# A first pass with constant mask rows and own scores apart, with four smaller edits, in a transformer block on one core

## The reference, in short

```
h = layernorm(x)*(1+ca) + sa
q, k, v = h @ w_qkv.T + b            # 16 heads of 8 dims
lines   = normalised exterior products of 4-dim projections (write: h[t-1], h[t]; read: h[t], h[t])
logits  = q.k/sqrt(8) + <read_line_q, J write_line_k> * decay_h**(q-k) * bias_scale_h   (second term for q > k)
x = x + ga * (softmax_causal(logits) @ v @ w_out.T + b_out)
h = layernorm(x)*(1+cb) + sb
x = x + gb * (top-2 of 8 experts, each 128 -> 256 (SwiGLU) -> 128, weighted by a softmax over the two)
```

## Time and profile before

| | us |
|---|---|
| three runs | 1112.86, 1106.92, 1110.35 |
| median | 1110.35 |
| profiled execution | 1111.9 |
| its span | 1110.2 |
| mean granted clock of TensorE | 0.955 |

### The profile page before, as it was taken

How to read it: one execution, slowest core, us unless ns; L and a number is a source line. 1 busy time by engine, 2 the same in 40 slices (tenths; PEclk the granted TensorE clock), 3 DMA queues, 4 the chain that set the end, 5 groups by cost and what they waited for, 6 DMA issues and landing times. The chain is left out here.

```text
span 1110.2 us, 30824 instructions
## 1 busy us (share of the span) xinstructions
PE 935.1 (84%) x9473; PEld 742.2 (67%) x9473; DVE 775.5 (70%) x2067; ACT 721.6 (65%) x1612; POOL 811.7 (73%) x1352
## 2 busy tenths in 40 slices
PE   2346899889999899998999989998872799999967
PEld 2335677767777777777777777776652688888852
DVE  8576668777777777777777777777746466555536
ACT  2435678887778877888787887876562455555520
POOL 8366668888888888888888888887435366666644
PEclk9997999999999999999999999998985899999989
DMA  7336556565666656666566665655411353333339
GB/s 189 114 110 161 150 139 172 152 178 137 168 159 158 172 147 160 161 158 173 143 163 159 153 178 146 163 156 157 118 44 49 79 168 93 91 91 91 83 138 357
DMA packets 233854, 160.39 MB, mean 144 GB/s; under 512 B 57376, under 2 KB 220512, under 8 KB 233568
## 3 DMA queue, kind: packets, MB, share of 16 engines
q1 hardware_dynamic: 222416, 133.77, 46.0%
q0 software_dynamic: 8448, 17.45, 5.1%
q10 hardware_dynamic: 2832, 7.20, 1.7%
HBM read 81.38 MB, written 76.19 MB: 142 GB/s over the span
## 5 line engine op out<-in xcount | busy, mean ns | idle before, releaser
L919 DVE TENSOR_REDUCE peak<-pre 128x6 f32<-128x768 f32 x256 | 244.5, 955 | 116.4 <-PE pre L759 113.5
L1151 ACT ACTIVATE PT<-sc 128x768 f32<-128x768 f32 x256 | 204.6, 799 | 35.3 <-PE sc L746 32.9
L950 DVE TENSOR_TENSOR sc<-sc,decay 128x512 f32<-128x512 f32 x256 | 177.5, 693 | 30.4 <-PE sc L730 25.3
L1637 POOL DMA_INDIRECT yab<-y_out,xt x136 | 131.4, 966 | 82.8 <-issue 63.4
L1359 POOL DMA_INDIRECT xg<-stage,slot_i x128 | 130.9, 1022 | 62.9 <-issue 26.8
L759 PE MATMUL pre<-causal,identb 128*128 128x256 bf16 x512 | 144.7, 283 | 0.0
L758 PE MATMUL pre<-KT,queries 84*128 84x256 bf16 x512 | 143.5, 280 | 0.0
L757 PE MATMUL pre<-KT,queries 84*128 84x128 bf16 x512 | 116.5, 228 | 20.4 <-DMA queries<-line_rows 12.6
L1591 DVE TENSOR_TENSOR hid<-silu,up 128x256 f32<-128x256 f32 x136 | 57.3, 421 | 82.0 <-ACT silu L1545 82.0
L743 PE MATMUL sc<-queries,KT 99*128 99x128 bf16 x512 | 101.6, 223 | 13.2 <-issue 6.8
L1545 ACT ACTIVATE silu<-up 128x256 f32<-128x256 f32 x136 | 52.2, 384 | 88.4 <-PE up L1481 88.4
(11 more groups left out here) (279 smaller groups left out, 2731.9 us busy)
## 6 DMA issues: line engine op xcount, KB each, us to landing
line_rows<-line_part SPq DMA_DIRECT2D x64, 216.0 KB
dim_rows<-dim_part SPq DMA_DIRECT2D x64, 192.0 KB, 2.1
KT<-dim_rows SPq DMA_DIRECT2D x64, 192.0 KB
queries<-dim_rows SPq DMA_DIRECT2D x64, 192.0 KB
line_rows<-line_part SPq DMA_DIRECT2D x64, 144.0 KB
KI<-line_rows SPq DMA_DIRECT2D x64, 144.0 KB
QI<-line_rows SPq DMA_DIRECT2D x64, 144.0 KB
xt<-xg SPq DMA_DIRECT2D x136, 65.0 KB, 1.9
```

The costliest lines, as they stand in the source:

```text
L919: nc.vector.reduce_max(peak[half][:, i:i + 2, 0:3], pre[:, :, 0:3 * P].rearrange("p n (g k) -> p n g k", g=3), AX.X)\
L950: nc.vector.tensor_tensor(seeded(p), seeded(p), decay[:, 2 * p:2 * p + 2, :].unsqueeze(2).broadcast_to([P, 2, NT, P]), ALU.mult).then_inc( ...
L1151: nc.scalar.activation(PT[p % 4][:], sc[:, window], ACT.Exp).then_inc(exped.sem, 1)
L1637: nc.gpsimd.indirect_dma_start(yab, bass.IndirectOffsetOnAxis(xt[r][:, D:D + 1].bitcast(i32), 0), y_out[r % 8][:], None).then_inc(y_sent[r ...
```

## The change

1. **First pass.** A new pair of tiles KB and QB (`first_rows`, not doubled by batch parity) holds 64 constant mask rows, set in the setup, and 48 rows of dims, loaded per half. The two diagonal blocks are products of QB and KB over these 112 rows; the block of later queries against earlier keys stays a product of QF and KT over rows 0:84. A head takes 3 x 128 columns; the matmul with the mask is gone. The score of a token with itself, which the mask rows leave out, is computed apart: DVE multiplies q and k (`own_part`, in attnT's tile, slot 4), a new job "self" (slot 6) sums the dims of a head by two small products with `head_of`, and DVE copies them beside the maxima (slot 7). `peak` has three tiles, and the last maximum (`peak_top`) runs over three values for both halves of the queries.
2. **Loads.** load_rows has two more DMAs of 192 KB, ahead of the four, and holds until the whole half's first pass is done. The peaks' rows are 84:87 of QF instead of 96:99.
3. **Residual.** Job res is two transposes; DVE adds the PSUM to x_all; ACT's copy is gone.
4. **Squares** run behind all evacuations of ACT's slot 4.
5. **Setup.** Six fills by DVE become two of half the length; POOL's fills of KT are fewer or half as long, its causal mask is gone; DVE has a second cast (KB beside KI), both early; ACT copies QB's mask rows.
6. **Pads.** The tile lies in first_rows and is filled by POOL behind the loop; the DMAs wait for it.

```diff
-    (6, 0, "back", -2, 1), (6, 1, "max0", 1, 0),
+    (6, 0, "back", -2, 1), (6, 1, "max0", 1, 0), (6, 2, "self", 3, 1),
...
                 for m in range(2):
-                    nc.vector.memset(v["KT"][m][32:64].rearrange("p h t -> p (h t)").bitcast(u32), 0)
-                    nc.vector.memset(v["QF"][m][32:64].rearrange("p h t -> p (h t)").bitcast(u32), 0)
-                    nc.vector.memset(v["QF"][m][64:96].rearrange("p h t -> p (h t)").bitcast(u32), 0)
+                    nc.vector.memset(pairs(v["QF"][m])[0:PEAK0, :, 0:P // 2], 0)
...
+                dve.wait_ge(key_mask_ok, 1)
+                for tile in ("KI", "KB"):
+                    nc.vector.tensor_copy(v[tile][0:MR].rearrange("p h (t k) -> p (h t) k", t=NT),
+                                          key_mask[1][:].unsqueeze(1).broadcast_to([MR, H * NT, P]))
...
-                    hold(pre_ready, jb - 1, 4 * half + 1)
+                    hold(pre_ready, jb - 1, 4 * half + 4)
                     heads, done = slice(8 * half, 8 * half + 8), rows_loaded[half].sem
+                    for kq, tile in ((0, KB), (1, QB)):
+                        sp.dma_start(tile[MR:PRE, heads, :], dim_rows[jb % 3][kq, :, heads, :]).then_inc(done, 16)
...
                 iterations(sp, body)
+                sp.wait_ge(pads_made, 2)
                 sp.dma_start(xg[E * CAP:XROWS, :].rearrange("(n p) d -> p n d", p=P), pads[:, 8:16, :]).then_inc(padded, 16)
...
-                        nc.tensor.matmul(pre[:, n, 0:P], QF[par][0:DIMS + LINES, h, 0:P], KT[par][0:DIMS + LINES, h, 0:P], start=True, stop=False)
-                        nc.tensor.matmul(pre[:, n, P:3 * P], QF[par][0:DIMS + LINES, h, P:T], KT[par][0:DIMS + LINES, h, :], start=False, stop=False)
-                        last = nc.tensor.matmul(diagonal(pre, n), identb[:], causal[:].unsqueeze(1).broadcast_to([P, 2, P]),
-                                                start=False, stop=True)
+                        first, second = slice(0, P), slice(P, T)
+                        nc.tensor.matmul(pre[:, n, 0:P], QB[0:PRE, h, first], KB[0:PRE, h, first], start=True, stop=True)
+                        nc.tensor.matmul(pre[:, n, P:T], QF[par][0:PEAK0, h, second], KT[par][0:PEAK0, h, first], start=True, stop=True)
+                        last = nc.tensor.matmul(pre[:, n, T:3 * P], QB[0:PRE, h, second], KB[0:PRE, h, second], start=True, stop=True)
...
                         wait(pe, used["out"], jb)
-                        settle(pe, pe_settled)
                         for t in range(NT):
                             blk = slice(t * P, (t + 1) * P)
-                            nc.tensor.matmul(B[:, blk], ident[:], x_all[:, span(jb * T + t * P, P)], start=True, stop=False)
-                            last = nc.tensor.matmul(B[:, blk], yT[:, blk], ident[:], start=False, stop=True)
+                            last = nc.tensor.transpose(B[:, blk], yT[:, blk], ident[:])
...
+                    elif name == "self":
+                        wait(pe, own_ready, jb)
+                        for t in range(NT):
+                            last = nc.tensor.matmul(B[:, t * H:(t + 1) * H], own_part[:, t * P:(t + 1) * P], head_of[:],
+                                                    start=True, stop=True)
...
                             if pp % 4 == 3:
                                 wait(dve, maxed, pb, 4 * half + 4)
-                                nc.vector.reduce_max(peak[half][:, :, 3], peak[half][:, :, 1:3], AX.X).then_inc(peaked.sem, 1)
+                                wait(dve, peak_step, pb - 1, 2 * half + 2)
+                                nc.vector.reduce_max(peak_top[half][:], mine[:, 8 * half:8 * half + 8], AX.X).then_inc(peaked.sem, 1)
...
+                    if p == 7 and live(b + 3):
+                        jb = b + 3
+                        wait(dve, ready["self"], jb)
+                        wait(dve, peaked, jb - 3, 2)
+                        own = bank[BANK["self"]][:, 0:NT * H].rearrange("p (t h) -> p h t", h=H)
+                        nc.vector.tensor_copy(peak[jb % 3][:].rearrange("p h t k -> p h (t k)")[:, :, 1:6:4], own)\
+                          .then_inc(used["self"].sem, 1)
...
                         jb = b + 3
+                        wait(dve, used["kq"], jb)
+                        wait(dve, ready["self"], jb - 1)
+                        wait(dve, ready["out"], jb - 4)
+                        nc.vector.tensor_tensor(own_part[:], dim_val[:, 0, :], dim_val[:, 1, :], ALU.mult).then_inc(own_ready.sem, 1)
                         wait(dve, squares, jb)
...
+                        wait(dve, ready["res"], jb)
+                        rows = x_all[:, span(jb * T, T)]
+                        nc.vector.tensor_tensor(rows, rows, bank[BANK["res"]][:, 0:T], ALU.add).then_inc(used["res"].sem, 1)
...
-                        if p == 4 and live(b + 3):
-                            squared(b + 3)
                         if p == 0 and live(b - 1):
...
                         if p == 4 and live(b - 2):
                             evacuate("norm2", b - 2, par)
+                        if p == 4 and live(b + 3):
+                            squared(b + 3)
...
                 iterations(pool, body)
+                wait(pool, pre_ready, NB - 1)
+                nc.gpsimd.memset(pads[:], 0.0).then_inc(pads_made, 1)
+                pool.wait_ge(pads_made, 1)
+                nc.gpsimd.iota(pads[:, :, D:D + 1].bitcast(i32), pattern=[[P, 16], [0, 1]], base=2 * NB * T,
+                               channel_multiplier=1).then_inc(pads_made, 1)
```

More of the change, by code:

```diff
@@ L33 @@
 INC = MR + LINES
+PRE = MR + DIMS
 LW = T + P
@@ L194, in build @@
         QI = a("QI", [P, H, T], bf16)
+        first_rows = a("first_rows", [P, 2, H, T], bf16)
+        KB, QB = (first_rows[:, n] for n in range(2))
+        pads = first_rows[:].rearrange("p n h t -> p (n h t)").bitcast(fp32)[:, 0:16 * ROW].rearrange("p (n d) -> p n d", d=ROW)
+        head_of = a("head_of", [P, H])
         VP = [a(f"VP{n}", [P, NT, H, 32]) for n in range(2)]
@@ L273, in _ @@
                                         pattern=[[-1, P]], channel_multiplier=1).then_inc(ident_ok, 1)
+                nc.gpsimd.memset(query_mask[0][:], MASK)
+                step(nc.gpsimd.memset(key_mask[0][:], 1.0))
+                nc.gpsimd.affine_select(out=key_mask[1][:], in_=key_mask[0][:], compare_op=ALU.is_ge, fill=0.0, base=-1,
+                                        pattern=[[1, P]], channel_multiplier=-2).then_inc(key_mask_ok, 1)
                 step(nc.gpsimd.iota(dist_i[:], pattern=[[1, P]], base=0, channel_multiplier=-1))
@@ L294, in _ @@
                 nc.gpsimd.tensor_copy(v["trib"][:], tri1[:])
[L295 to L302, removed]
                 nc.gpsimd.wait_ge(ident_ok, 1)
@@ L365, in _ @@
                 nc.scalar.activation(lz[:], ez[:], ACT.Ln, bias=1.0).then_inc(ln_ok, 1)
+                act.wait_ge(query_mask_ok, 1)
+                nc.scalar.activation(v["QB"][0:MR].rearrange("p h (t q) -> p (h t) q", t=NT),
+                                     query_mask[2][:].unsqueeze(1).broadcast_to([MR, H * NT, P]), ACT.Copy)
                 act.wait_ge(ld_v, 64)
@@ L478, in attend @@
         hT = [a(f"hT{n}", [P, T + 1]) for n in range(2)]
-        peak = [a(f"peak{n}", [P, 8, 4]) for n in range(2)]
+        peak = [a(f"peak{n}", [P, H, NT, 3]) for n in range(3)]
+        peak_top = [a(f"peak_top{n}", [P, 8, NT]) for n in range(2)]
         peak_rest = a("peak_rest", [P, NT, 8])
@@ L914, in body @@
                         if live(pb):
-                            half, i = pp // 4, 2 * (pp % 4)
+                            half, mine = pp // 4, peak[pb % 3]
                             wait(dve, pre_ready, pb, pp + 1)
-                            if pp % 4 == 0:
-                                wait(dve, peak_step, pb - 1, 2 * half + 2)
-                            nc.vector.reduce_max(peak[half][:, i:i + 2, 0:3],
+                            nc.vector.reduce_max(mine[:, 2 * pp:2 * pp + 2].rearrange("p n t k -> p n (t k)")[:, :, 2:5],
                                                  pre[:, :, 0:3 * P].rearrange("p n (g k) -> p n g k", g=3), AX.X)\
@@ L1056, in _ @@
                 nc.vector.memset(three_halves[:], 1.5)
+                for n in range(3):
+                    nc.vector.memset(peak[n][:, :, 0, 0:1], MASK)
                 for n in range(2):
@@ L1103, in evacuate @@
                         wait(act, dim_rested, jb - 1)
+                        wait(act, own_ready, jb - 1)
                         for n in range(2):
@@ L1122, in evacuate @@
                         nc.scalar.activation(peakT[half][:], B[0:24, 0:T], ACT.Copy, scale=-1.0).then_inc(done, 1)
-                    elif name == "res":
-                        nc.scalar.activation(x_all[:, span(jb * T, T)], B[:, 0:T], ACT.Copy).then_inc(done, 1)
                     elif name == "attnT":
+                        wait(act, ready["self"], min(jb + 3, NB - 1))
```

(4 more changed lines are left out.)

50 lines of the change are left out of this document (24 added, 26 removed).

## The result

The changed kernel takes 1239.56 us (median of four runs, 1237.04 to 1242.90) against 1109.1 before: a ratio of 1.117 (95% interval 1.113 to 1.122), 130 us slower, far above the range given. The profiled execution has a span of 1235.3 us and a mean granted clock of 0.828.

A forecast was written before the change was run, and what follows sets the result against it. The prediction took POOL to pace the loop from about batch 5 to 28, with PE having some 2.5 us to spare. Terms -2.5 + 4 + 4 + 6 + 3 + 4.7 = +19.2 gave 1129.5 us, range 1098 to 1160.

The forecast's parts named there:

- +6 of the steady stage: Steady batches: lateness 1.2 plus 0.1, less 1.04 to spare, is 0.25 a batch; over 24 batches +6 us, ends 0 and +30.
- I take 1.2: Added row loads: rows land later by 0.7 (issues alone) to 2.1 us (bytes); 1.2 taken, nearer the issues.
- 1.04 to spare: Steady batch: the half's peaks are ready at 419.43 and POOL splits them at 420.47, leaving 1.04 us.
- none of the slack reaches: Upper end of the steady stage's term: the rows' lateness costs 1.25 us a batch, +30 in all.
- inside the 1.04 above: Squares in a batch: they start about 0.65 us later; DVE's reduction and the weighing move by that, within POOL's slack.
- 3 x 1.4: Squares in the fill: each starts some 1.4 us later in three passes of a chain, +4 us, ends 0 and +6.
- Worth 0 in the steady stage: First pass: PE saves some 2 us of a batch that POOL paces, so 0 gained in the steady stage.
- Setup: Fewer, shorter zero fills and early casts in the setup: -2.5 us, ends -5.9 and -1.2.
- The faster one: Rival: the added rows land within the slack, landing moving by less than about 0.5; -9.4 us, or 1101; chance 0.20.
- POOL hid 0.9 of it: Rival judged here: POOL hides all lateness in the steady stage and the ends cancel; +3.5 us, 1114; chance 0.18.
- The clock: Rival: PE idles longer, its clock falls once in each of 24 steady batches; +15 on the forecast, 1145; chance 0.12.
- A blocked POOL: Rival: DVE's new product stops POOL for 0.35 us in each of 32 batches; +11 us, 1141; chance 0.08.

The follow-up runs named there:

- e6: The kernel before with the residual added by VectorE and nothing else: 1104.8 us, ratio 0.995.
- e1: The changed kernel without the two added row loads per half, their rows zeroed once in the setup: 1148.6 us, ratio 1.034.
- e13: The changed kernel with the two added loads of each half issued ahead of that half's peaks, same bytes: 1156.2 us, ratio 1.039.
- e5: The kernel before with the squares behind the evacuations of ACT's slot 4 and nothing else: 1145.5 us, ratio 1.029.
- e12: The changed kernel with the squares in front again, as before the change: 1236.0 us, ratio 1.112.
- e14: The changed kernel with the added loads issued ahead of the half's peaks and the squares in front again: 1135.9 us, ratio 1.020.
- e3: The changed kernel with the first pass of before and the two added loads going into tiles that nobody reads: 1289.0 us, ratio 1.164.
- e4: The changed kernel with the first pass and the loads of before, all other edits kept: 1139.8 us, ratio 1.026.
- e11: The kernel before with the residual on VectorE and the setup's edits, without the other three: 1103.6 us, ratio 0.995.
- e8: The kernel before with the setup's edits alone, the fill of the pads staying in the setup: 1116.9 us, ratio 1.006.
- e2: The changed kernel with two more matmuls of 128 columns per head in the first pass, loads as changed: 1267.4 us, ratio 1.141.
- e10: The changed kernel with eight more matmuls of 512 columns on PE in the wait for half 1's rows: 1235.4 us, ratio 1.113.

## Why the prediction was wrong

**The bound, right as far as it went.** PE was not the bound: with half a microsecond less PE work per batch (e6) the period stayed. That POOL paced the loop is what its even gaps say; no run tested it by itself. But a second loop ran beside it, rows, first pass, peaks, split, peak load, rows, with hardly any room, and I gave that loop's lateness only one measure.

**The step that failed** is the one that made +6 of the steady stage: "I take 1.2", "1.04 to spare", "0.25 a batch". Measured: half 1's first use comes 2.2 us later behind the issue, just above the upper end of my bounds (2.1, the bytes at the rate of the stretch); as PE waited for these rows in only 2 of the 22 batches before and in all of them after, the landing itself is late by at least that. That "the loads of one half have their stretch almost to themselves" was the wrong reason to go below 2.1. And the 1.04 was POOL's distance to one pair of peaks, not the room of the loop, which closes over the next row load: the steady stage pays 3.7 a batch, three times what I had priced as "none of the slack reaches". 2.2 of it is the landing, 1.5 the way back. In the way back POOL's slack did take up 0.9 (2.8 to 1.9 ahead of the split), but from the first to the last slot of the half it takes 1.6 longer and the product behind the split comes 0.8 later, terms that I did not have. The way back is as long without the added loads (19.0 in e1), so the loads' own part is the landing. With the loads' bytes off that way (e13) 83 us of the 130 are gone.

**The squares** were the second failed step: "inside the 1.04 above". The delay goes another way than through the peaks: norm_sq stands ahead of the weighing on DVE's queue, PE's scores wait for that (e5), and the way back is 1.5 longer with them alone. The prediction did name what stands behind the reduction and then priced it by the wrong slack. In the changed kernel this is hidden by the row loads of both halves (e12); it comes to light when the added ones are moved (e14). In the fill the term was right: the third square runs at 88.97 in e5 and at 84.92 before, 4.05 later where 3 x 1.4 was forecast, and 2.4 of that reach the first scatter.

**The short first pass**, priced at nothing, is worth 49 us together with its own scores once the rows' loop sets the pace (e3 against the changed kernel), and without the loads the new pass with its own scores costs 9 (e1 against e4; 3.8 of it is e1's longer setup, as far as that reaches the end). "Worth 0 in the steady stage" held only while POOL paced.

**Setup**: the term was right in size (-2.5; its end came 2.7 earlier in the changed kernel) but brought nothing by itself: alone it ended 6 to 8 us slower, in its trace with more time at the lower clock. That the edits themselves bring this is not shown, since with the residual (e11) it doesn't appear; why the falls came so in e8 stays open.

**Fill and early batches**: the first scatter is 14 us later, where the terms gave +5.5 with the setup; the rows' landing is the larger part there as well (PE waits 1.9 to 3.9 for half 1's rows in each of batches 0 to 5). With the added loads early the first scatter comes at 182.0 (e13), without them at 182.6 (e1): 10 to 11 of the 14 us are the loads'. The fill's clock is low in the changed kernel (0.61 from 31 to 95 us against 0.93), but e6 has 0.68 there and an earlier first scatter than before.

**Last batches** (+3): the three periods between first scatters in which rows are still loaded are 14.0 us longer together (75.4 against 61.4), the same late rows as in the steady stage; the three behind them are 3.9 shorter.

**Pads**: +5.9 without the residual; the first load of the experts stands 13.0 behind the last scatter's issue (974.96 to 987.96) instead of 6.0, +7.0. Right, slightly small.

**The rivals.** The faster one fell with the landing: 2.2, not under 0.5. POOL hid 0.9 of it and no more. The clock did fall in nearly every batch, as that rival said, but not for its reason (e2: more work doesn't help), and the time hardly follows the clock while the rows set the pace (e10). A blocked POOL does show in the changed kernel's trace, but small. In six steady batches an addition of POOL's that takes 0.20 elsewhere starts just after the start of DVE's new product (own_part, in attnT's tile) and ends some 0.05 us after the product's end; one of them (DVE's timeline, then POOL's):

```profile
245.41 0.41 DVE L1013 TENSOR_TENSOR attnT<-dim_val 128x256 f32<-128x256 f32 x1
```

```profile
245.47 0.41 POOL L1372 TENSOR_TENSOR run<-run,hot_sum 128x8 bf16<-128x8 bf16 x1
```

With three more in the fill and the early batches this is some 1.7 us over the whole kernel, where the rival had 11. In most batches the product meets a scatter of POOL's, which is hardly longer for it (1.10 to 1.16), a gap, or an operation that began ahead of it.

## What to carry to other kernels

Where two loops have nearly the same length, a trace shows the slack of the one that waits, not its room over a whole turn: add the edit's delay to the loop's own length (issue to use, use to next issue) and compare with the period. A load between two dependent steps is priced at least by its bytes at the rate of that stretch, not by its issue (here 2.1 us by the bytes, 2.2 measured); and one whose source and target are ready earlier belongs ahead of the wait, as e13 shows (83 us by moving two calls). Moving one instruction behind others on its queue is not free because the engine was idle: ask which engine's queue waits for it.

## What the runs showed that was not expected

TensorE's clock fell behind a wait of 1.9 to 3.6 us per batch even though PE was busy 4.7 to 5.0 of the 5 us ahead of it: some 10 us of each 27 at 1.2 GHz (an estimate from the mean of 0.81). Filling part of that wait raised the mean clock from 0.81 to 0.89 and gained nothing, because PE then waited for the other half's rows; so a low clock in the profile was here a sign of the late rows more than the price paid for them. And the DMA engines, with as large a busy share (0.73), moved 182 GB/s with the loads spread out and 167 with six together.
